# A four-layer stack on one core: biased attention written out over its eight pairs of heads, a state scan with its work moved between engines, and stages whose first loads are put in another order

## The chip, the cores and the metric

The program runs on 1 core of one Trainium2 chip. The metric is the device time of one execution in microseconds (us); lower is better. The engines are TensorE (PE; PEld is its weight load), VectorE (DVE), ScalarE (ACT), GpSimd (POOL) and SyncE (SP, which issues DMAs here, as ACT's queue does too).

## The reference, cut to what matters

Eight sublayers follow each other on 4 x 1024 tokens of width 256, each as x = layernorm(x + f(x)). Four of them touch the change.

```
# L1 attention (stage Catt): 16 heads of width 16, not causal, no mask; bias by distance
P = softmax(q k^T * scale + rel_emb[bucket(mem - ctx)]);  o = P v
# L0 attention (stage Aatt): the same without bias, causal.
# L0 and L3 "ffn" (stages B0*, B1*, H0*, H1*): two layers each of rotary, windowed attention
# (8 heads of width 64, window 128) and a gated MLP.
# L2 attention (stage scan):
phi = k_val[..., None] * theta;  re_k = cos(phi);  im_k = sin(phi)
num_re = cumsum(p_w * re_k);     num_im = cumsum(p_w * im_k)
out_re = sum_m(num_re * qr + num_im * qi) * inv
# L3 attention (stage lru): h_t = lam * h_{t-1} + gamma * B x_t with complex lam, as a scan;
# it needs tables cos(n w), sin(n w) for n < 1024, worked out from a log that is an input.
```

## The kernel before, in words

The program is a chain of 30 stages, one function call each. A stage has its own tiles and semaphores, writes its result to HBM, and ends with a barrier over all engines, so nothing of the next stage runs before the last instruction of this one, and what a stage loads first it loads with every engine idle. Inside a stage each engine has its own program, and waits on semaphores for the others. `pipelined(eng, count, steps, parts)` writes such a program: the parts run in each step with their lags, iteration 0 is written out as instructions with constants, iterations 1 to count-1 are one hardware loop (`Fori`), whose waits take their values from registers, and the lagging parts of the last iteration are written out behind it.

**Thin attention** (`stage_thin_attention`; Aatt without bias, Catt with it). An iteration is a pair of heads, 8 in all, with 64 steps: 4 batches x 2 heads x 8 tiles of 128 query rows. In a step PE makes scores of 128 rows against all keys (L1094), DVE adds the window of biases and takes the negated row maximum (L1155, one per step, into `Catt_nmax`); 24 steps later PE makes the scores again by key with the maximum and the far biases as extra rows of the contraction (L1116), DVE adds the near biases for the blocks beside the diagonal (L1179), ACT takes exp (L1216), and PE sums the values three steps later (L1137). Once in 16 steps the maxima are split in three bf16 parts, turned by PE (L1104), and sent through HBM into rows 96 to 98 of Q. SP loads Q, K, V, and for Catt the extra rows of K (`ext`), `near` and the `win`dows. At the start of the stage POOL fills V and K[96:99] with ones, makes tables and an identity, and raises `set_up`; SP, PE and DVE wait for that, and SP for Catt also for three DMAs (`put`) of the table `of` into Q. One semaphore `head_in` per batch counts all its loads.

**Local attention** (`stage_local_attention`, four stages): the same way, `head_in` counts q, k and V; scores use q and k alone, V comes in five steps later. **Rotary qkv** (`stage_qkv_rotary`, four stages): SP loads the weights w, then the rotary tables and six small rows of scales, all on `w_in`, and then the activations `hT` in the loop; PE and DVE wait for all of `w_in`.

**The state scan** (`stage_state_scan`): 64 steps (4 batches x 2 groups x 8 tiles). In a step DVE makes the phase `ph` (L2353) and its rounded value `nn` (L2357), POOL the fraction f = ph - nn (L2275), ACT |f|, sin and cos (L2323, L2324, L2326), DVE weighs the sines (L2362) and POOL the cosines (L2280), PE runs the two cumulative sums by 16 matmuls of 512 columns (8 where a group starts; L2304, L2306), DVE multiplies both sums by the queries (L2373, twice), POOL adds the products (L2287), DVE reduces (L2378) and scales (L2381). `ph`, `nn`, `f`, `ys` lie in SBUF; only `cum` is in PSUM.

**The recurrence** (`stage_recurrence`, lru): DVE first builds the tables of sines from the logs, a chain of about 130 small instructions ending in L2772, and only then starts on the states (L2783), for which PE has the inputs (L2693).

Of the kernel before, what the change touches and what calls it, by code (L numbers as in the profile page):

```python
# [25 lines left out]
P = 128  # L26
B = 4
# [51 lines left out]
def pipelined(eng, count, steps, parts):  # L79
# [17 lines left out]
    for i in range(steps, steps + max(lag for lag, _ in parts)):  # L97
        run(count - 1, i)

# [187 lines left out]
def stage_enter(nc, x, act0, acts):  # L287

    with ExitStack() as ctx:
        pl = Pool_(nc, ctx, "enter")  # L290
        xin = pl.sb("xin", [P, IN, C])
# [46 lines left out]
        def _(s):  # L338
# [3 lines left out]
            with s.Fori(0, B) as it:  # L342
                for u in range(NT):
# [6 lines left out]
                                xt[:, si, :].rearrange("p (k t) -> p k t", k=KT)).then_inc(cols_out[si], 16)  # L350
            for i in range(IN):
                s.wait_ge(cols_out[i], 16 + 16 * B * NT // IN)

# [267 lines left out]
def stage_local_attention(nc, name, q_s, k_s, v_s, r_s, oT_s, scale):  # L621
# [6 lines left out]
    with ExitStack() as ctx:  # L628
# [14 lines left out]
        head_in = [pl.sem(f"head_in{i}") for i in range(B)]  # L643
# [27 lines left out]
        def _(sp):  # L671
            def load(it, b):
                sp.wait_ge(pv_done, it * ST + (b + 1) * NT)
                apart(sp, pl.sp_unread)
                for i, x in enumerate((q_s, k_s)):
                    sp.dma_start(qk[:, b, i, :], x[bass.ds(it * P, P), b * T:(b + 1) * T]).then_inc(head_in[b], 16)
                sp.dma_start(V[:, b], v_s[b * T:(b + 1) * T, bass.ds(it * P, P)].rearrange("(t p) d -> p t d", p=P)
                             ).then_inc(head_in[b], 16)
# [36 lines left out]
        def _(t):  # L715
# [191 lines left out]
def stage_thin_attention(nc, name, q_s, k_s, v_s, nm_s, r_s, oT_s, scale, bias=None):  # L907
# [6 lines left out]
    causal = bias is None  # L914
    PAIRS, hd, GS, LAG, PRIMED = 8, 16, 16, 24, 16
# [4 lines left out]
    LOADS = 4 if causal else 6  # L920
# [40 lines left out]
    with ExitStack() as ctx:  # L961
# [16 lines left out]
        ident_made, set_up, put = pl.sem("ident_made"), pl.sem("set_up"), pl.sem("put")  # L978
        head_in = [pl.sem(f"head_in{i}") for i in range(B)]
# [19 lines left out]
        def _(sp):  # L999
            sp.wait_ge(set_up, 1)  # L1000
            if not causal:
# [5 lines left out]
                sp.wait_ge(put, 16 * PARTS)  # L1007
# [6 lines left out]
            def load(it, b):  # L1014
                if b == 1 and not causal:
                    window(it, 0)
                sp.wait_ge(pv_done, it * nv + (b + 1) * (nv // B))
                apart(sp, pl.sp_unread)
                for x, x_s in ((Q, q_s), (K, k_s)):
                    sp.dma_start(x[0:K0, b], x_s.rearrange("f t c -> (f t) c")[bass.ds(it * (2 * K0), 2 * K0), b * T:(b + 1) * T]  # L1020
                                 .rearrange("(h p) c -> p h c", h=2)).then_inc(head_in[b], 16)
                for h in range(2):
                    sp.dma_start(V[:, b, :, h, 0:hd], v_s[b * T:(b + 1) * T, bass.ds(it * (2 * hd) + h * hd, hd)]
                                 .rearrange("(t p) d -> p t d", p=P)).then_inc(head_in[b], 16)
                if not causal:
                    sp.dma_start(K[K0 + PARTS:K1, b], ext[bass.ds(it * (2 * PARTS * NT), 2 * PARTS * NT), :]
                                 .rearrange("(h p) c -> p h c", h=2)).then_inc(head_in[b], 16)
                    sp.dma_start(near[:, b], nears[bass.ds(it * (2 * P), 2 * P), :].rearrange("(h p) c -> p h c", h=2)
                                 ).then_inc(head_in[b], 16)
                if b == 1 and not causal:  # L1030
                    window(it, 1)

# [14 lines left out]
        def _(g):  # L1047
            g.memset(V[:], 1.0)
            g.drain()
            g.memset(K[K0:K0 + PARTS], 1.0)  # L1050
            g.drain()
            if causal:
                CausalWindow().make(g, win[:, 0, :])
                g.drain()
# [26 lines left out]
        def _(t):  # L1081
            t.sem_inc(pv_done, nv)
            t.sem_inc(m_turned, 2)
            t.wait_ge(set_up, 1)

            def scores(it, j):
                b, (h, u) = j // GS, row_of(j)
                if j % GS == 0:
                    t.wait_ge(head_in[b], it * (16 * LOADS) + 16 * LOADS)
# [7 lines left out]
            def turn_maxima(it, j):  # L1097
# [3 lines left out]
                n = behind_sums(b)  # L1101
                t.wait_ge(split_done, it * B + (b + 1))
# [4 lines left out]
            def scores_by_key(it, i):  # L1107
                b, h, kb = i // GS, i % 2, i % GS // 2
                if i % GS == 0:
                    t.wait_ge(max_in[b], it * 16 + 16)  # L1110
                if (i + LAG - 3) % GS == GS - 1 and not (isinstance(it, int) and it == PAIRS - 1 and b == B - 1):
# [29 lines left out]
            pipelined(t, PAIRS, ST, ((0, scores), (3, turn_maxima), (LAG, scores_by_key), (LAG + 3, values)))  # L1141

        @block.vector
        def _(v):
            v.sem_inc(masked, ST)
            v.wait_ge(set_up, 1)
# [24 lines left out]
            def add_near(it, i):  # L1171
                b, h, kb = i // GS, i % 2, i % GS // 2
                for c, lo, hi, n, some in units[i]:
# [15 lines left out]
            pipelined(v, PAIRS, ST, ((LAG, add_near), (0, mask), (LAG + 9, invert)))  # L1189
# [1755 lines left out]
```

## Time and profile before

| | |
|---|---|
| time, 3 runs | 8263.17 us median (8258.72 to 8267.3) |
| the profiled execution | 8261.89 us, of it 8260.2 us span |
| busy in the span | PE 82%, DVE 59%, ACT 33%, POOL 19% |
| stage Aatt | 282.3 to 1061.9 us |
| stages B0qkv, B1qkv, H0qkv, H1qkv | from 1173.4, 2011.6, 6559.0 and 7409.6 us, 224 to 226 us each |
| stages B0att, B1att, H0att, H1att | from 1400.6, 2240.2, 6786.7 and 7637.2 us, 243 to 257 us each |
| stage Catt | 3169.7 to 4385.9 us |
| stage scan | 4961.2 to 5588.9 us |
| stage lru | 6337.3 to 6556.5 us |

A share of the span is an average over 30 stages that have different bounds, so the stage must be read, not the total. In the rows below a time is in us from the start of the span; PEclk 1.00 is the clock of 2.4 GHz and 0.50 that of 1.2 GHz. In brackets behind an instruction stands the idle time of its engine before it and what ended it; "issue" is idle time that no other engine or DMA explains.

### The profile page before, as it was taken

The page shows a single profiled execution, that of the slowest core. Times are in us where ns is not written, and L with a number is a line of the kernel's source. Part 1 is how long each engine was busy: PE and PEld are TensorE (multiplying, and loading weights), DVE is VectorE, ACT ScalarE, POOL GpSimd, SP SyncE. Part 2 cuts the span into 40 slices and gives each one's busy share as a digit, 9 for nine tenths or more (in the row PEclk, how much of TensorE's full clock was granted, in tenths as well). Part 3 has the DMA queues.
Part 4 walks back from the last instruction along what each step waited for, and adds up shares of the span by engine and source line. Part 5 has one row for each costly group of instructions (what it writes and reads, how often), then busy time and mean ns, then how long its engine had stood idle before and what let it go on. Part 6 is the DMA issues. An engine that isn't in the chain of part 4 may idle for free. (4 is left out here: it accounts for less than half of the span.)

```text
span 8260.2 us, 122768 instructions
## 1 busy us (share of the span) xinstructions
PE 6734.6 (82%) x30724; PEld 3442.2 (42%) x30724; DVE 4886.6 (59%) x12027; ACT 2733.4 (33%) x6003; POOL 1566.9 (19%) x847
## 2 busy tenths in 40 slices
PE   6799958988898866999994486776886689889989
PEld 3233334554465432222223352334443345544554
DVE  3555557634774535777775749994334676337645
ACT  0255524612471101555551113331110146124621
POOL 1111115100510011000000007880000261006100
PEclk9899979999999987999997698998988899999999
DMA  5322244542454274222223221103001345424541
GB/s 177 95 60 59 52 131 146 172 136 73 149 173 146 81 250 115 72 64 66 64 49 105 82 75 41 30 25 114 23 30 32 101 149 169 139 71 138 172 153 55
DMA packets 921871, 833.01 MB, mean 101 GB/s; under 512 B 239752, under 2 KB 786528, under 8 KB 921248
## 3 DMA queue, kind: packets, MB, share of 16 engines
q1 hardware_dynamic: 491920, 505.95, 21.2%
q10 hardware_dynamic: 429568, 323.08, 12.5%
q14 instruction: 280, 2.29, 0.1%
q8 instruction: 103, 1.69, 0.1%
HBM read 486.33 MB, written 345.74 MB: 101 GB/s over the span
## 5 line engine op out<-in xcount | busy, mean ns | idle before, releaser
L1216 ACT ACTIVATE Catt_E<-Catt_t 128x512 f32<-128x512 f32 x1024 | 576.8, 596 | 501.6 <-DVE Catt_t L1179 319.7
L1155 DVE CUSTOM_DVE_ANT_0 Catt_S<-Catt_s,Catt_win 128x1024 f32<-128x1024 f32 x512 | 621.3, 1215 | 40.9 <-DMA Catt_win<-skewed 38.8
L1155 DVE CUSTOM_DVE_ANT_0 Aatt_S<-Aatt_s,Aatt_win 128x128 f32<-128x128 f32 (+7 forms) x512 | 377.2, 756 | 325.7 <-PE Aatt_s L1094 320.0
L1137 PE MATMUL Catt_o<-Catt_E,Catt_V 128*32 128x256 f32 (+1 forms) x3840 | 548.6, 404 | 0.0
L1216 ACT ACTIVATE Aatt_E<-Aatt_t 128x512 f32<-128x512 f32 (+3 forms) x768 | 355.4, 489 | 325.5 <-PE Aatt_t L1119 257.4
L1179 DVE TENSOR_TENSOR Catt_t<-Catt_t,Catt_near 128x256 f32<-128x256 f32 (+2 forms) x640 | 281.2, 456 | 261.6 <-PE Catt_t L1116 229.9
L1116 PE MATMUL Catt_t<-Catt_Q,Catt_K 123*128 123x512 bf16 x1024 | 327.9, 388 | 91.9 <-ACT Catt_E L1216 71.8
L1094 PE MATMUL Catt_s<-Catt_K,Catt_Q 96*128 96x512 bf16 x1024 | 324.4, 400 | 46.8 <-DMA Catt_near<-near_s 38.1
L2304 PE MATMUL scan_cum<-scan_X,scan_after 128*128 128x512 f32 x448 | 251.3, 644 | 121.8 <-DVE scan_pr L2373 117.5
L1137 PE MATMUL Aatt_o<-Aatt_E,Aatt_V 128*32 128x256 f32 (+2 forms) x2304 | 324.5, 389 | 0.0
L2306 PE MATMUL scan_cum<-scan_X,scan_upto 128*128 128x512 f32 x512 | 279.0, 637 | 39.5 <-POOL scan_X L2280 23.5
L1137 PEld LDWEIGHTS Catt_o<-Catt_E,Catt_V 128*32 128x32 f32 x3840 | 180.3, 110 | 272.0 <-issue 184.3
L1078 POOL TENSOR_TENSOR Catt_O<-Catt_O,Catt_Rb 64x1024 f32<-64x1024 f32 x32 | 75.4, 2357 | 1126.2 <-DMA Catt_Rb<-r_s 1126.2
L1116 PE MATMUL Aatt_t<-Aatt_Q,Aatt_K 99*128 99x512 bf16 (+3 forms) x768 | 241.8, 333 | 48.4 <-ACT Aatt_E L1216 23.6
L1094 PE MATMUL Aatt_s<-Aatt_K,Aatt_Q 96*128 96x512 bf16 (+3 forms) x768 | 219.4, 342 | 42.9 <-DMA Aatt_V<-v_s 26.4
L2275 POOL TENSOR_TENSOR scan_f<-scan_ph,scan_nn 128x1024 f32<-128x1024 f32 x64 | 208.3, 3255 | 46.3 <-DVE scan_nn L2357 46.3
L1116 PEld LDWEIGHTS Catt_t<-Catt_Q,Catt_K 123*128 123x128 bf16 x1024 | 99.4, 98 | 282.3 <-ACT Catt_E L1216 185.4
L1078 POOL TENSOR_TENSOR Aatt_O<-Aatt_O,Aatt_Rb 64x1024 f32<-64x1024 f32 x32 | 75.1, 2347 | 690.5 <-DMA Aatt_Rb<-r_s 690.5
L2323 ACT ACTIVATE scan_ab<-scan_f 128x1024 f32<-128x1024 f32 x64 | 67.7, 1057 | 408.0 <-POOL scan_f L2275 408.0
L2304 PEld LDWEIGHTS scan_cum<-scan_X,scan_after 128*128 128x128 f32 x448 | 86.7, 204 | 256.1 <-issue 232.9
L2580 DVE TENSOR_TENSOR moe_hid<-moe_sg,moe_u 128x512 f32<-128x512 f32 x80 | 54.3, 686 | 223.9 <-ACT moe_sg L2519 223.9
L1094 PEld LDWEIGHTS Catt_s<-Catt_K,Catt_Q 96*128 96x128 bf16 x1024 | 59.3, 98 | 298.3 <-issue 263.2
(724 smaller groups left out, 15070.5 us busy)
## 6 DMA issues: line engine op xcount, KB each, us to landing
bias_rows<-line SPq DMA_DIRECT2D x16, 960.0 KB
skewed<-bias_win ACTq DMA_DIRECT2D x16, 960.0 KB, 5.9
Catt_win<-skewed SPq DMA_DIRECT2D x16, 960.0 KB, 4.7
rec<-state_in_r ACTq DMA_DIRECT2D x32, 416.0 KB, 2.4
scan_r<-rec SPq DMA_DIRECT2D x64, 208.0 KB
Aatt_Q<-q_parts SPq DMA_DIRECT2D x32, 384.0 KB
Aatt_K<-k_parts SPq DMA_DIRECT2D x32, 384.0 KB
Catt_Q<-q_parts SPq DMA_DIRECT2D x32, 384.0 KB
```

The source lines that it names most:

```text
L1078: g.tensor_tensor(o, o, half(Rb, b), ALU.mult).then_inc(o_scaled, 1)
L1094: ins = t.matmul(s_ps[j % 2][:, c:d], Q[0:K0, b, h, u * P:(u + 1) * P], K[0:K0, b, h, c:d], start=True, stop=True)
L1116: ins = t.matmul(t_ps[n % 2][:, 0:hi - lo], K[:, b, h, kb * P:(kb + 1) * P], Q[:, b, h, lo:hi], start=True, stop=not diagonal)
L1137: ins = t.matmul(o_ps[f:f + 2 * hd, x:y], V[:, b, kb, h, :], E[:, kb % NB, h, x:y], start=kb == 0, stop=kb == end and y == hi)
L1155: v.tensor_tensor_reduce(out=S[:, j % 2, 0:w], in0=s_ps[j % 2][:, 0:w], in1=win[:, 0 if causal else h, w0:w0 + w], scale=-1.0, scalar=BIG, ...
L1179: v.tensor_tensor(x, x, near[:, b, h, a - (kb - 1) * P:z - (kb - 1) * P], ALU.add).then_inc(near_done, 1)
L1216: a.activation(E[:, kb % NB, h, lo:hi], t_ps[n % 2][:, 0:hi - lo], ACT.Exp, scale=scale).then_inc(exped, 1)
L2275: g.tensor_tensor(f[:, j % 2, :], ph[:, j % 2, :], nn[:, j % 2, :], ALU.subtract).then_inc(f_done, 1)
L2304: t.matmul(cum[i][:, c:c + 512], after[:], X[:, (j - 1) % 4, i, c:c + 512], start=False, stop=False, skip_group_check=True)
L2306: ins = t.matmul(cum[i][:, c:c + 512], upto[:], X[:, j % 4, i, c:c + 512], start=u == 0, stop=True, skip_group_check=True)
L2323: a.activation(ab[:], f[:, s, :], ACT.Abs)
L2580: ins = v.tensor_tensor(h, sg[:, k % 2, :], u_ps[k % 2][:], ALU.mult)
```

## The change

(1) For Catt, PE, DVE and ACT no longer use `pipelined` but `written_out`: all 512 steps are instructions with constant waits, with no hardware loop. SP and POOL keep their loops, and Aatt keeps `pipelined` on all engines. (2) Thin attention starts differently: K's ones are set by DVE, not POOL; the semaphore `head_in` counts only Q and K, `late_in` the rest; SP no longer waits for `set_up`; for Catt the first window is loaded right behind Q and K of batch 0 and the `put` DMAs are issued behind the second window. (3) Local attention waits for V on its own semaphore. (4) Rotary qkv loads w, then the first two `hT` pieces, then the tables, which have their own semaphore `r_in` that DVE alone waits for. (5) The recurrence's tables are built in the first stage (enter), where DVE had nothing to do, and stay in SBUF; ACT makes the two sines there between batch 0 and batch 1. (6) The scan: `ph` and `ys` go to PSUM; the rounding is an ACT instruction (`whole`, with a bias of 12582912), the fraction a DVE instruction that reads `nn` and the PSUM `ph`; POOL keeps the weighing, one step later and behind DVE's, and the add; the imaginary sum goes first.

```diff
+def written_out(eng, count, steps, parts):
+    for i in range(count * steps + max(lag for lag, _ in parts)):
+        for lag, fn in parts:
+            if 0 <= i - lag < count * steps:
+                fn((i - lag) // steps, (i - lag) % steps)
# stage_enter
+            tables.load(sp, logs)
...
-            with s.Fori(0, B) as it:
+            columns(0)
+            tables.sines(s)
+            with s.Fori(1, B) as it:
+                columns(it)
# stage_local_attention
-                    t.wait_ge(head_in[b], it * 48 + 48)
+                    t.wait_ge(head_in[b], it * 32 + 32)
...
+                if u == 0:
+                    t.wait_ge(V_in[b], it * 16 + 16)
# stage_thin_attention
+    run = pipelined if causal else written_out
...
-            sp.wait_ge(set_up, 1)
-                sp.wait_ge(put, 16 * PARTS)
...
+                if b == 0 and not causal and isinstance(it, int):
+                    window(it, 0)
+                if b == 0 and isinstance(it, int):
+                    sp.wait_ge(V_ones, 1)
...
                 if b == 1 and not causal:
                     window(it, 1)
+                    if isinstance(it, int):
+                        put_of()
...
-            g.memset(K[K0:K0 + PARTS], 1.0)
-            t.wait_ge(set_up, 1)
-                    t.wait_ge(head_in[b], it * (16 * LOADS) + 16 * LOADS)
+                    t.wait_ge(head_in[b], it * 32 + 32)
+                if b == 0 and isinstance(it, int):
+                    t.wait_ge(set_up, 1)                 # before the maxima are turned
+                if i == 0 and isinstance(it, int):
+                    t.wait_ge(K_ones, 1)                 # before the scores by key
+                        t.wait_ge(put, 16 * PARTS)
+                    t.wait_ge(late_in[b], it * (16 * LATE) + 16 * LATE)
-            pipelined(t, PAIRS, ST, ((0, scores), (3, turn_maxima), (LAG, scores_by_key), (LAG + 3, values)))
+            run(t, PAIRS, ST, ((0, scores), (3, turn_maxima), (LAG, scores_by_key), (LAG + 3, values)))
-            v.wait_ge(set_up, 1)
+            v.memset(K[K0:K0 + PARTS], 1.0).then_inc(K_ones, 1)
# stage_qkv_rotary
+            columns(0, 0)
+            sp.dma_start(rt[:], rot.rearrange("(t p) a d -> p t a d", p=P)).then_inc(r_in, 16)
...
+            columns(0, 1)
-            t.wait_ge(w_in, 16 * 8)
+            t.wait_ge(w_in, 16)
-            v.wait_ge(w_in, 16 * 8)
+            v.wait_ge(r_in, 16 * 7)
# stage_state_scan
+        ph = pl.ps("ph", (P, W))
+        ys = [pl.ps(f"ys{i}") for i in range(2)]
-            pipelined(g, B, ST, ((1, weigh), (0, fraction), (2, add)))
+            pipelined(g, B, ST, ((2, weigh), (3, add)))
-                    for i in range(2):
+                    for i in (1, 0):
+            def whole(it, j):
+                a.wait_ge(ph_done, n + 1)
+                a.wait_ge(f_done, n + 1)
+                a.activation(nn[:, j % 2, :], ph[:], ACT.Identity, bias=magic[:]).then_inc(rounded, 1)
-            pipelined(a, B, ST, ((0, trig), (3, store)))
+            pipelined(a, B, ST, ((1, trig), (0, whole), (4, store)))
+            def fraction(it, j):
+                v.wait_ge(rounded, n + 1)
+                v.wait_ge(trig_done, n + 1)
+                v.scalar_tensor_tensor(out=f[:, j % 2, :], in0=nn[:, j % 2, :], scalar=-MAGIC, in1=ph[:],
+                                       op0=ALU.add, op1=ALU.subtract).then_inc(f_done, 1)
             def phase(it, j):
+                v.drain()
...
-                v.drain()
-                v.tensor_scalar(nn[:, j % 2, :], ph[:, j % 2, :], MAGIC, -MAGIC, ALU.add, ALU.add).then_inc(ph_done, 1)
-            pipelined(v, B, ST, ((0, phase), (1, weigh), (2, read), (3, reduce)))
+            pipelined(v, B, ST, ((1, fraction), (0, phase), (2, weigh), (3, read), (4, reduce)))
# stage_recurrence: L2729 to L2773 (exp of the logs, the doubling of the tables) go to
# RecurrenceTables.make(v), which stage_enter's DVE program calls; q.wait_ge(trig_done, 2) goes.
```

## Rows read from the trace of the kernel before

**Rows 1.** Windows: stage Catt and stage scan; busy us (count) of each engine, clock, DMA.

```profile
3169.00:4386.00 1217.00, 1071.33 (x5920) 342.02 (x5920) 886.93 (x1824) 617.39 (x1089) 87.95 (x40) 0.95 0.26 62
4961.00:5589.00 628.00, 464.71 (x960) 191.11 (x960) 598.16 (x449) 203.19 (x193) 503.46 (x197) 0.92 0.11 30
```

**Rows 2.** Timeline: DVE in one step of the scan, and the next step's first.

```profile
5259.61 1.21 DVE L2353 TENSOR_TENSOR scan_ph<-scan_th,scan_r 128x1024 f32<-128x1024 f32 x1
5260.90 2.23 DVE L2357 TENSOR_SCALAR scan_nn<-scan_ph 128x1024 f32<-128x1024 f32 x1
5263.05 1.21 DVE L2362 TENSOR_TENSOR scan_X<-scan_sn,scan_r 128x1024 f32<-128x1024 f32 x1
5264.18 1.21 DVE L2373 TENSOR_TENSOR scan_pr<-scan_cum,scan_r 128x1024 f32<-128x1024 f32 x1
...
5267.80 1.32 DVE L2381 TENSOR_TENSOR scan_y<-scan_ys,scan_r 128x128 f32<-128x128 f32 x1
5269.04 1.21 DVE L2353 TENSOR_TENSOR scan_ph<-scan_th,scan_r 128x1024 f32<-128x1024 f32 x1
```

**Rows 3.** Timeline: POOL in the same step.

```profile
5260.36 2.21 POOL L2280 TENSOR_TENSOR scan_X<-scan_cs,scan_r 128x1024 f32<-128x1024 f32 x1 [0.83 <-ACT scan_cs L2326]
...
5266.60 2.37 POOL L2287 TENSOR_TENSOR scan_pr<-scan_pr,scan_pi 128x1024 f32<-128x1024 f32 x1
```

**Rows 4.** Windows: that step; PE, PEld, DVE, ACT, POOL.

```profile
5259.60:5269.00 9.40, 7.07 (x17) 2.96 (x16) 9.18 (x8) 3.11 (x4) 7.85 (x3) 1.00 0.11 30
```

**Rows 5.** Timeline: the scan's first steps, DVE and ACT.

```profile
4968.73 0.69 DVE L2357 TENSOR_SCALAR scan_nn<-scan_ph 128x1024 f32<-128x1024 f32 x1
...
4973.91 1.28 ACT L2324 ACT_TABLE_LOAD   x1
```

**Rows 6.** Timeline: DVE and PE where pair 1 of Catt jumps back to pair 2.

```profile
3463.25 0.63 DVE L1179 TENSOR_TENSOR Catt_t<-Catt_t,Catt_near 128x128 f32<-128x128 f32 x2 [5.16 <-issue]
...
3464.32 1.09 PE L1116 MATMUL Catt_t<-Catt_Q,Catt_K 123*128 123x512 bf16 x2 [5.41 <-ACT Catt_E L1216]
```

**Rows 7.** Windows of the tile Catt_S alone: DVE busy (count), clock, DMA.

```profile
3287.00:3321.00 34.00, 19.43 (x16) 1.00 0.34 86
3355.20:3389.70 34.50, 19.43 (x16) 1.00 0.26 55
3424.20:3463.70 39.50, 19.42 (x16) 0.97 0.36 98
3321.00:4330.00 1009.00, 544.07 (x448) 0.98 0.26 62
```

**Rows 8.** DMA queues from 3205 to 3321, pair 0 of Catt: transfers, MB, share.

```profile
q8 instruction: 4, 0.07, 0.2%
q14 instruction: 4, 0.03, 0.1%
```

**Rows 9.** Timeline: start of Catt, SP's queue and DVE.

```profile
3198.50 0.38 SPq L1012 DMA_DIRECT2D Catt_win<-skewed  x1
...
3205.48 1.23 DVE L1155 CUSTOM_DVE_ANT_0 Catt_S<-Catt_s,Catt_win 128x1024 f32<-128x1024 f32 x1 [38.75 <-DMA Catt_win<-skewed]
```

**Rows 10.** Timeline: start of Aatt, POOL and DVE.

```profile
284.21 6.92 POOL L1050 MEMSET Aatt_K<- 3x8192 bf16 x1
...
302.86 0.82 DVE L1155 CUSTOM_DVE_ANT_0 Aatt_S<-Aatt_s,Aatt_win 128x640 f32<-128x640 f32 x1 [23.55 <-PE Aatt_s L1094]
```

**Rows 11.** Start of B1qkv: windows, then PE's first in the timeline.

```profile
2012.00:2018.00 6.00, 0.00 (x0) 0.00 (x0) 0.00 (x0) 0.00 (x0) 0.29 (x1) 0.50 0.90 302
...
2026.04 1.19 PE L1536 MATMUL B1qkv_qk<-B1qkv_w,B1qkv_hT 128*128 128x512 f32 x1 [19.44 <-DMA B1qkv_hT<-cols]
```

**Rows 12.** Timeline: PE's first in B0att.

```profile
1411.03 1.23 PE L729 MATMUL B0att_s<-B0att_qk 64*128 64x128 f32 x6 [14.78 <-DMA B0att_V<-v_s]
```

**Rows 13.** Timeline: start of lru, PE's inputs and DVE's first states.

```profile
6344.94 5.37 PE L2693 MATMUL lru_u<-lru_xc,lru_b 128*128 128x512 f32 x7 [12.98 <-DMA lru_xc<-cols]
...
6373.18 1.41 DVE L2783 SCALAR_TENSOR_TENSOR lru_m<-lru_u,lru_ex,lru_rot 128x512 f32<-128x512 f32 x2 [0.17 <-issue]
```

More of the change, by code:

```diff
@@ L977, in stage_thin_attention @@
         o_ps = pl.ps("o", (P, T))
-        ident_made, set_up, put = pl.sem("ident_made"), pl.sem("set_up"), pl.sem("put")
-        head_in = [pl.sem(f"head_in{i}") for i in range(B)]
+        ident_made, V_ones, K_ones, win_made, set_up, put = (pl.sem(n) for n in ("ident_made", "V_ones", "K_ones", "win_made", "set_up", "put"))
+        head_in, late_in = ([pl.sem(f"{n}{i}") for i in range(B)] for n in ("head_in", "late_in"))
         max_in = [pl.sem(f"max_in{i}") for i in range(B)]
@@ L999, in _, with put_of @@
         def _(sp):
-            sp.wait_ge(set_up, 1)
-            if not causal:
+            def put_of():
                 sp.wait_ge(of_made, 1)
@@ L1014, in load @@
             def load(it, b):
-                if b == 1 and not causal:
+                if b == 1 and not causal and not isinstance(it, int):
                     window(it, 0)
@@ L1047, in _ @@
         def _(g):
-            g.memset(V[:], 1.0)
-            g.drain()
-            g.memset(K[K0:K0 + PARTS], 1.0)
+            if causal:
+                CausalWindow().make(g, win[:, 0, :]).then_inc(win_made, 1)
+                g.drain()
+            g.memset(V[:], 1.0).then_inc(V_ones, 1)
             g.drain()
             if causal:
-                CausalWindow().make(g, win[:, 0, :])
-                g.drain()
                 g.memset(near[:], 0.0)
@@ L1172, in add_near @@
                 b, h, kb = i // GS, i % 2, i % GS // 2
+                if i % GS == 0 and not causal:
+                    v.wait_ge(late_in[b], it * (16 * LATE) + 16 * LATE)
                 for c, lo, hi, n, some in units[i]:
@@ L1187, in invert @@
                 v.reciprocal(sums[:, b % 2], sums[:, b % 2]).then_inc(inverted, 1)
-            pipelined(v, PAIRS, ST, ((LAG, add_near), (0, mask), (LAG + 9, invert)))
+            run(v, PAIRS, ST, ((LAG, add_near), (0, mask), (LAG + 9, invert)))
         @block.scalar
@@ L1473, in stage_qkv_rotary @@
         tr_ps = [pl.ps(f"tr{i}") for i in range(2)]
-        made, w_in, tabled = pl.sem("made"), pl.sem("w_in"), pl.sem("tabled")
+        made, w_in, r_in = (pl.sem(n) for n in ("made", "w_in", "r_in"))
         h_in = [pl.sem(f"h_in{i}") for i in range(2)]
@@ L2261, in _ @@
             g.memset(quarter[:], float(np.pi / 2))
+            g.memset(magic[:], MAGIC)
             g.drain()
@@ L2621, in stage_recurrence @@
+def stage_recurrence(nc, act_in, tables, bre, bim, cre, cim, d, out):
     with ExitStack() as ctx:
@@ L2735, in _ @@
-            v.drain()
-            v.tensor_scalar(n3[:, 0:1], n3[:, 0:1], -MAGIC, None, ALU.add)
-            v.drain()
-            rest = ex[:, 1:2]
-            for part in (6.28125, 0.0019350051879882812, float(2 * np.pi - 6.28125 - 0.0019350051879882812)):
-                v.scalar_tensor_tensor(out=wr[:], in0=n3[:, 0:1], scalar=-part, in1=rest, op0=ALU.mult, op1=ALU.add)
-                v.drain()
-                rest = wr[:]
-            v.tensor_scalar(wr[:], wr[:], 3.1415925, -3.1415925, ALU.min, ALU.max)
@@ L2775, in _ @@
-            v.drain().then_inc(trig_done, 1)
             def states(it, c):
@@ L2828, in local_transformer @@
         return y
-    stage_enter(nc, i["L0_attn_x"], a0, acts)
+    kept = ExitStack()
+    tables = RecurrenceTables(nc, kept)
+    stage_enter(nc, i["L0_attn_x"], a0, acts, tables, i["L3_logs"])
     cur = a0
```

190 lines of the change are left out of this document (107 added, 83 removed).

## The prediction, made before the change was run

> **What bounds it now.** I read the timeline for the starts and ends of the stages first, since 30 stages with a barrier between them simply add up, and the change touches twelve of them. The others should keep their times. Next the windows of the two large ones [rows 1]: in Catt PE is busy 1071 of 1217 us and DVE 887; in the scan DVE 598 of 628, PE 465, POOL 503, ACT 203. So Catt belongs to PE and the scan to DVE, and neither share says what the engine does with its time. The timeline of one scan step [rows 2] does: from one `ph` to the next, 9.43 us, with DVE busy 9.18 [rows 4]. Two of its instructions are too long for what they do. `nn` has one operand of 1024 elements and takes 2.23 us, but 0.69 in the first step, when POOL has no work yet [rows 5]; POOL's product `X` runs from 5260.36 to 5262.57, over `nn` [rows 3]. `y`, 128 elements, takes 1.32 while POOL's add runs until 5268.97. So DVE waits inside its instructions for POOL. The products that read `cum` in PSUM take 1.21 beside the same POOL [rows 2]. In Catt I looked at the masks (tile `Catt_S`), 16 to a group [rows 7]: a written-out group takes 34.00 us, a looped one 34.50, and one that holds the jump back 39.50, where DVE and PE both stand for 5 us with nothing that the profile can name [rows 6]. Last, the first work of each stage and what ended the wait ahead of it [rows 9 to 13].
>
> **The scan.** Starts of successive DVE products are 1.13 apart (5263.05 to 5264.18 [rows 2]). From the first `pr` to `y` 3.62 pass; without two reads at 1.13, reduce with its drain has 1.36. A new DVE step is then fraction 1.21, phase 1.13, weigh 1.13, two reads 2.26, reduce 1.36 and `y` 0.25 (128 of 1024 elements of 1.13, and some start, an estimate as its row is a blocked one): 7.34, say 7.4. `nn` leaves DVE, the fraction comes. Does POOL still block it? Fraction, reads and `y` have an operand in PSUM, the kind that row 2 shows unblocked. POOL's product now waits for DVE's weigh, so it lies beside the reads; its add follows the reads and needs 2.4, over reduce, `y` and fraction (2.8). Phase starts just behind it.
> The Trainium skill, SBUF — State Buffer, section "SBUF: two separate sides", says that a DVE instruction in its fast mode or with two SBUF inputs and a GpSimd one exclude each other for a whole instruction. The trace agrees with it for `nn` (2.23 against 0.69); by that rule no pair is left here but phase and weigh, with the sum unchanged.
> The other engines: PE is busy 7.07 in the step [rows 4], now under DVE's 7.4; POOL 2.21 + 2.37 = 4.6 [rows 3]; ACT 3.11 [rows 4] and the new `whole`, some 1.05 (a third of 3.11). The circle fraction, |f| and sines, `whole`, next fraction is 1.21 + 3.11 + 1.05 and some 0.5 of handing over, 5.9. So DVE still sets the step: 64 x (9.43 - 7.4) = 130, less 5 for one more lag to fill: **-125**. Bounds: all six large ones at 1.13 give 7.03, 64 x 2.4 - 5 = -149; -61 is the rival below.
>
> **Catt written out.** Pairs 1 to 7 took 1009.0 for 28 groups [rows 7]. Written-out code shows 34.00; the looped groups next to it 34.50, of which some may be PE's own and stay. I take 34.2: 28 x 34.2 = 958, **-51** (34.0: -57; 34.5: -43). That is 8.5 for each of the six jumps: 5.0 in the group itself (39.50 - 34.50) and the rest behind it, in the looped code's 0.3 a group and in the groups after a jump.
> The Trainium skill, Runtime: NRT & Kernel Launch, section "Instruction fetch mechanics", says that a taken branch out of the held pages must fetch before it goes on, and that straight code is fetched ahead. The rows on the jump agree; by that rule all six go.
>
> **Catt's front.** The first mask waits for `win`, issued at 3198.50 and used at 3205.48 [rows 9], 7 later. The stage starts at 3169.7. SP now waits for nothing, issues Q and K (0.4 each) and the window at some 3171.1, and the first mask is due at 3178 to 3180 against 3205.5: **-26** (20 to 27). What is late next: the `put` DMAs stand in SP's queue behind the second window, so behind the loads of batches 0 and 1, and should land by 3195. PE needs the maxima's parts from step 19 and `put` from step 24; at 34/16 = 2.1 a step that is 3219 and later. DVE's memset of K's ones takes POOL 6.92 [rows 10], at most that on DVE, and lies beside the window's load.
>
> **Aatt's front.** There POOL's two fills stood ahead of SP, and the first mask came 20.6 after the start, at 302.86 [rows 10]. Now Q and K land some 5 after it, and DVE's memset (5 to 6.9) ends at 287.5 to 289.5: mask at some 288.5, **-14.5** (11 to 15).
>
> **Rotary qkv, four times.** The loads run at 302 GB/s with the queues 0.90 busy, mean of the first 6 us, and PE starts at 2026.04, 14.4 after the stage [rows 11]. By their shapes w is 1.57 MB and the first `hT` pieces 0.5: 2.1 MB at 302 is 7 us from 2012, some 2019, PE from 2020.5: -5.5 each. DVE needs the tables for its first product later, and its multiply by the scales then comes about when PE's first results do; if it is late, some is lost: 3.5 to 6.5. **-22** (14 to 26).
>
> **Local attention, four times.** PE's first waited for V [rows 12]. Without V it needs Q and K; at least one issue (0.4), at most 3.5 of V's small rows. I take 2.5: **-10** (1.6 to 14).
>
> **lru.** The states start at 6373.18; the inputs they need are there behind seven or eight matmuls, 6344.94 + 5.37 = 6350 [rows 13]. POOL and ACT had been waiting for the same chain. **-23.5** (20 to 24).
>
> **enter.** ACT paces that stage (63 us) and gets a table load (1.28 [rows 5]) and two short sines, SP one issue of 0.4 ahead: **+2.5** (1 to 4). The doubling of the tables, about 30 us of small DVE instructions, is hidden there, where DVE had nothing; without that cover lru's 23.5 would come back here.
>
> Sum: -125 - 51 - 26 - 14.5 - 22 - 10 - 23.5 + 2.5 = -269.5. The profiled execution took 8261.9, so 7992.4; it lies 1.3 below the median of the runs, so **7994** for those.
>
> **Rivals.** (a) *The scan gets another bound.* ACT gets `whole` behind the sines; a table load is 1.28 [rows 5], and if |f| or `whole` lies in another table, each step has two: the circle is 5.9 + 2.56 = 8.4, over DVE's 7.4. Two DVE instructions blocked for half a us each by POOL would do as much. Gain 64 x (9.43 - 8.4) - 5 = 61 and not 125: 8058. Against: ACT's four instructions per step with |f| among them are busy 3.11 in all [rows 4], so |f| loads nothing. For: phase starts only 0.4 behind the end of POOL's add.
> The Trainium skill, ScalarE: Activation LUTs, section "Table sets: the hidden batching unit", has abs, copy and identity in every set; by that, `whole` loads nothing, and rows 4 agree for |f|.
> (b) *The fronts give nothing*, since the loads are as fast as the queues are (0.90 busy [rows 11]) and the first steps merely wait at another place. Then scan and Catt's jumps alone count, 176: 8087. Against: in Catt, Aatt and lru the wait was for POOL's fills and DVE's chain, not for a transfer's length.
> (c) *Slower: written-out code must be fetched.* Pair 0, which is written out, took 8 instruction fetches [rows 8], so seven more pairs take 56. If each stopped its engine as a jump does, 8.5 with what follows, that were 476: 8263 - 270 + 476 = 8469; it turns the sign from 270/56 = 4.8 each. Against: groups of pair 0 with such fetches took 34.00, the shortest of all [rows 7]. Only if the fetches for PE, DVE and ACT fell behind after pair 0 would this come.
>
> **Numbers.** The main case has 0.64, (a) 0.21, (b) 0.08, (c) 0.03; 0.04 is for more than the bounds allow. The main case's own range is 7952 (all bounds at their best: 149 + 57 + 27 + 15 + 26 + 14 + 24 - 1 = 311) to about 8045 (the scan at 100, the rest at half way to their lower bounds). The range given reaches over (a) to (b): 7950 to 8086. Below 0.2%, 16.5 us, a measurement of this kernel can hardly tell a change from none; only (c) and a stumble inside it come near: faster 0.96, same 0.01, slower 0.03.
>
> **What would show it.** In the scan: `ph` to `ph` 7.4 on DVE, no instruction of it over 1.4, no table load but the first; 8.4 with loads is (a). In Catt: groups of 34.0 to 34.2 throughout, no 5 us of "issue"; groups of 36 and more with fetches inside are (c). First masks 9 after Catt's start and 6 after Aatt's; PE's first 9 after a rotary stage's start and 8 after a local one's; lru's states 13 after its start; enter ending at 66.6. I would be wrong above all if DVE's step were longer for reads of PSUM by two engines at once, or if PE, at half clock after any stall, became the slower one in the scan (7.07 of 7.4 is little room).

## The result and the profile after

The changed kernel takes 7997.63 us, median of 4 runs (7994.45 to 7999.97); before it was 8263.94 in the same series. The ratio is 0.9678, 95% interval 0.9661 to 0.9695. The profiled execution took 7999.97. The forecast was 7994, range 7950 to 8086.

Since the stages only add up, the comparison is made stage by stage. A stage is counted here from its first instruction to the first of the next one, in the timelines of before and after; "forecast" is the term of the prediction.

| stage | before | after | difference | forecast |
|---|---|---|---|---|
| enter | 65.8 | 61.9 | -3.9 | +2.5 |
| Aatt | 782.5 | 773.7 | -8.9 | -14.5 |
| four rotary qkv | 911.1 | 886.4 | -24.7 | -22 |
| B0att | 249.4 | 245.9 | -3.5 | -2.5 |
| B1att | 246.3 | 257.6 | +11.3 | -2.5 |
| H0att, H1att | 521.2 | 513.0 | -8.2 | -5 |
| Catt | 1219.1 | 1139.6 | -79.5 | -77 |
| scan | 630.3 | 510.5 | -119.8 | -125 |
| lru | 221.7 | 202.2 | -19.5 | -23.5 |
| moe (the experts, not edited) | 644.2 | 624.0 | -20.2 | 0 |
| the other 16 stages, not edited | 2767.8 | 2782.7 | +14.9 | 0 |

So the total is right to 4 us, but partly by luck: a stage that nobody edited gave 20, one that should gain lost 11. In these two traces the edited stages give 256.7 together, where 269.5 were forecast, and the unedited ones 5.3. About half of moe's 20 and the whole of B1att's 11 turn out to have one cause, which the prediction did not have (below). Of the 14.9 in the other 16 stages, 9.5 lie in the stage just ahead of the scan; it takes 246.5 to 254.7 in the traces of the kernels below, with the same code, so they may be chance.

First the scan. The timeline of one step after the change, DVE, with ACT's new instruction and POOL's product and add:

```profile
5099.64 1.23 DVE L2407 TENSOR_TENSOR scan_ph<-scan_th,scan_r 128x1024 f32<-128x1024 f32 x1
5100.78 1.22 DVE L2414 TENSOR_TENSOR scan_X<-scan_sn,scan_r 128x1024 f32<-128x1024 f32 x1
5101.92 1.22 DVE L2425 TENSOR_TENSOR scan_pi<-scan_cum,scan_r 128x1024 f32<-128x1024 f32 x1
5102.08 1.90 POOL L2319 TENSOR_TENSOR scan_X<-scan_cs,scan_r 128x1024 f32<-128x1024 f32 x1 [2.79 <-DVE scan_X L2414]
...
5102.94 1.11 ACT L2361 ACTIVATE scan_nn<-scan_ph,scan_magic 128x1024 f32<-128x1024 f32 x1
...
5104.34 2.35 POOL L2326 TENSOR_TENSOR scan_pr<-scan_pr,scan_pi 128x1024 f32<-128x1024 f32 x1 [0.36 <-DVE scan_pr L2425]
5105.47 0.29 DVE L2433 TENSOR_TENSOR scan_y<-scan_ys,scan_r 128x128 f32<-128x128 f32 x1
5105.68 1.21 DVE L2400 SCALAR_TENSOR_TENSOR scan_f<-scan_nn,scan_ph 128x1024 f32<-128x1024 f32 x1
...
5106.98 1.23 DVE L2407 TENSOR_TENSOR scan_ph<-scan_th,scan_r 128x1024 f32<-128x1024 f32 x1
```

From `ph` to `ph` 7.34 us, where it was 9.43 [rows 2]. `y` takes 0.29, not 1.32, though POOL's add runs from 5104.34 to 5106.69 over it, and the fraction takes 1.21 under the same add. Nothing on DVE in this step is longer than 1.23 (in the whole stage two instructions are: one `ph` of 2.31 in the first steps and one `X` of 2.09 near the end), and the stage has one table load. The windows (busy us and count of PE, PEld, DVE, ACT, POOL; clock; DMA), in the order Catt, scan, that step, a longer one, against [rows 1, 4]:

```profile
3160.00:4299.60 1139.60, 1054.05 (x5920) 337.95 (x5920) 890.46 (x1825) 617.12 (x1089) 81.02 (x39) 0.97 0.28 67
4880.00:5391.00 511.00, 437.97 (x960) 182.27 (x960) 465.10 (x449) 274.41 (x257) 273.48 (x134) 0.95 0.13 37
5102.00:5109.50 7.50, 7.15 (x18) 3.00 (x17) 7.33 (x8) 4.42 (x5) 4.33 (x3) 1.00 0.14 38
5159.20:5168.30 9.10, 8.23 (x20) 3.53 (x19) 8.69 (x10) 4.39 (x5) 5.55 (x3) 1.00 0.15 36
```

PE is busy 7.15 of 7.5, so it has become a near second bound, and in seven of the 63 steps it is the first: they take 8.8 to 9.4. PE's timeline at one of them (a start of a group of tiles), and the windows that say what clock it was granted:

```profile
5148.03 2.08 PE L2343 MATMUL scan_cum<-scan_X,scan_after 128*128 128x512 f32 x2 [3.75 <-DVE scan_pi L2425]
5149.90 1.75 PE L2345 MATMUL scan_cum<-scan_X,scan_upto 128*128 128x512 f32 x2
5151.48 1.02 PE L2343 MATMUL scan_cum<-scan_X,scan_after 128*128 128x512 f32 x2
```

```profile
5143.00:5148.00 5.00, 1.28 (x3) 0.21 (x2) 4.91 (x6) 3.37 (x4) 2.13 (x2) 0.99 0.20 56
5148.00:5151.50 3.50, 3.47 (x5) 1.52 (x6) 3.43 (x4) 0.90 (x1) 3.21 (x2) 0.52 0.00 0
5152.00:5158.00 6.00, 6.00 (x16) 2.65 (x15) 4.49 (x5) 4.04 (x4) 1.90 (x1) 1.00 0.10 35
5088.40:5091.90 3.50, 3.42 (x8) 1.63 (x9) 3.43 (x4) 0.85 (x1) 3.14 (x2) 1.00 0.00 0
```

Where a group of tiles starts PE has 8 matmuls and not 16. It stands 3.75 us, and behind that the granted clock is 0.52 (1.2 GHz) for 3.5 us, two matmuls take 2.08 and not 1.02, and in the step after, DVE's `pr` waits 1.51 for the sums. PE stands 3.7 to 3.8 us at seven group starts of the stage. Behind six of them the granted clock is 0.53 to 0.67 for the next 3.5 us, and the step takes 9.1 to 9.4; behind the seventh, at 5088.48 (last row), the clock stays at 1.00 and the step takes 7.45. So, as far as these seven show, what costs is the clock behind the stand and not the stand itself; why it stayed up once is open. (The seventh long step, 8.8, is at the very start of the stage.)

Catt: two groups of masks (the windows of tile `Catt_S`), the last of pair 0 and the one that held the first jump before, against [rows 7]:

```profile
3255.40:3289.30 33.90, 19.37 (x16) 1.00 0.35 87
3391.20:3425.30 34.10, 19.43 (x17) 1.00 0.34 86
```

All groups of pairs 1 to 7 take 33.8 to 34.6. The fronts, in DVE's timeline of Catt and then of Aatt, against [rows 9, 10]:

```profile
3161.88 6.88 DVE L1178 MEMSET Catt_K<- 3x8192 bf16 x1 [4.85 <-issue]
3168.88 1.23 DVE L1189 CUSTOM_DVE_ANT_0 Catt_S<-Catt_s,Catt_win 128x1024 f32<-128x1024 f32 x1
...
3183.60 1.22 DVE L1189 CUSTOM_DVE_ANT_0 Catt_S<-Catt_s,Catt_win 128x1024 f32<-128x1024 f32 x1 [4.79 <-DMA Catt_win<-skewed]
```

```profile
283.28 6.88 DVE L1178 MEMSET Aatt_K<- 3x8192 bf16 x1 [4.93 <-issue]
290.20 0.82 DVE L1189 CUSTOM_DVE_ANT_0 Aatt_S<-Aatt_s,Aatt_win 128x640 f32<-128x640 f32 x1
```

In both stages the fill of K's ones, 6.88 us on DVE as it was 6.92 on POOL, ends just ahead of the first mask: what the prediction hid behind the loads is now the last thing that the mask waits for. In Catt the ninth mask also waits 4.79 for the second window.

The surprise is in B1att, in DVE's timeline before and after at the same point of the program, the jump back from one pair to the next. Before, the work goes on:

```profile
2357.70 0.69 DVE L668 COPY B1att_PT<-B1att_pt 128x512 f32<-128x512 f32 x1 [0.31 <-PE B1att_pt L741]
2358.38 0.29 DVE L782 CUSTOM_DVE_ANT_0 B1att_S<-B1att_s,B1att_win 128x128 f32<-128x128 f32 x1
```

After the change it doesn't:

```profile
2333.18 0.69 DVE L687 COPY B1att_PT<-B1att_pt 128x512 f32<-128x512 f32 x1 [0.31 <-PE B1att_pt L760]
2339.47 0.29 DVE L803 CUSTOM_DVE_ANT_0 B1att_S<-B1att_s,B1att_win 128x128 f32<-128x128 f32 x1 [5.59 <-issue]
```

This loop was not edited; its body is 350 DVE instructions in both. What changed is how much DVE code lies ahead of it: enter now holds the tables' chain. What DVE waits for is code. The queue listing of the second round, from one jump to the next, shows no transfer of instructions before:

```profile
q1 hardware_dynamic: 6859, 11.26, 63.9%
```

and after the change, for the same round:

```profile
q1 hardware_dynamic: 6791, 11.01, 57.4%
q14 instruction: 5, 0.04, 0.2%
```

One of those five starts inside the first jump, at 2337.22, and one more, at 2399.35, inside the second. So before, the loop ran its round without fetching anything, and after the change every round fetches, with DVE standing at the jump.

### The profile page after: what moved, and what is told of

Read it like the earlier page. It is cut to its first block and busy times, and to the rows that moved or that the text cites. A ratio compares the mean times of both kernels' runs of the same rounds, so it can differ in the third digit from the quotient of the medians.

```text
span 7998.3 us, 119081 instructions
## 1 busy us (share of the span) xinstructions
PE 6696.7 (84%) x30724; PEld 3430.9 (43%) x30724; DVE 4761.2 (60%) x12029; ACT 2802.8 (35%) x6066; POOL 1323.1 (17%) x782
## 5 line engine op out<-in xcount | busy, mean ns | idle before, releaser
L1148 PE MATMUL Catt_t<-Catt_Q,Catt_K 123*128 123x512 bf16 x1024 | 321.6, 382 | 51.8 <-ACT Catt_E L1252 33.8
L2528 PE MATMUL moe_g<-moe_xc,moe_wg 128*128 128x512 f32 x320 | 166.6, 645 | 0.0
L2345 PEld LDWEIGHTS scan_cum<-scan_X,scan_upto 128*128 128x128 f32 x512 | 99.3, 195 | 154.7 <-issue 151.8
L2326 POOL TENSOR_TENSOR scan_pr<-scan_pr,scan_pi 128x1024 f32<-128x1024 f32 x64 | 150.8, 2356 | 40.0 <-DVE scan_pr L2425 40.0
```

Of the source, the lines that this page charges most:

```text
L1148: ins = t.matmul(t_ps[n % 2][:, 0:hi - lo], K[:, b, h, kb * P:(kb + 1) * P], Q[:, b, h, lo:hi], start=True, stop=not diagonal)
L2326: g.tensor_tensor(pr[:, m % 2, :], pr[:, m % 2, :], pi[:, m % 2, :], ALU.add).then_inc(sum_done, 1)
L2345: ins = t.matmul(cum[i][:, c:c + 512], upto[:], X[:, j % 4, i, c:c + 512], start=u == 0, stop=True, skip_group_check=True)
L2528: ins = t.matmul(ps[k % 2][:], w[:, kt, j * P:(j + 1) * P], xc[:, c, kt, :], start=kt == 0, stop=kt == KT - 1)
```

## The experiments

Times are medians. The kernel before took 8253 to 8264 in the different series, so differences under 10 us between kernels of different series are judged by the stage in the trace; the ratios to before stand where the total matters. There is one trace of each kernel. A stage with the same code differs by some us from trace to trace: Aatt takes 772.2 to 776.6 in those that leave it as the change has it, the scan 509.2 to 513.4, Catt 1138.7 to 1141.3.

**Which engine's jump?** In Catt PE, DVE and ACT are put back on `pipelined` together, DVE alone, or PE and ACT without DVE.

```diff
-            run(v, PAIRS, ST, ((LAG, add_near), (0, mask), (LAG + 9, invert)))
+            pipelined(v, PAIRS, ST, ((LAG, add_near), (0, mask), (LAG + 9, invert)))
```

All three looped: 

> The changed kernel with one part undone: in stage Catt PE, DVE and ACT loop over the pairs again; scan and fronts stay new. In the changed kernel's trace the 28 groups of pairs 1 to 7 take 950 us in place of 1009, so the theory that the jumps and the looped code were worth this everywhere expects 7998 + 59 = 8057 (8050 to 8062), with six groups of 39.5 again. The rival, that part of the gain came from the new front (other places of the loads against the groups), expects clearly less, 8030 or below.

DVE alone: 

> The changed kernel with DVE alone looping over the pairs in Catt; PE and ACT stay written out. In the trace before, DVE shows 5.1 us from the branch to its next instruction, ACT 2.7, PE 0.2, and PE's wait was ended by ACT, which waited for DVE. Theory: DVE's jump alone is what the stage pays; then this costs nearly all of it, 8050 to 8057, groups with the jump at 39.5. Rival: every engine's jump adds its part; then it lies at half or less, 8020 to 8035. What the other groups take (34.5 or 34.0) tells whose looped waits the 0.5 was.

PE and ACT: 

> The counterpart: PE and ACT loop over the pairs in Catt, DVE alone is written out. Theory (DVE's jump is the one that counts): 7998 to 8010, no group over 36, since ACT's 2.7 and PE's 0.2 fit into what the buffers between the engines hold. Rival (every jump adds): ACT's 2.7 with the half clock behind it six times and the looped groups' 0.5 give 8020 to 8035.

Measured 8061.15, 8056.85 and 8002.67 (one of the last kernel's four executions took 8103). Catt itself took 1193.2, 1187.5 and 1148.5 against 1139.6: +53.6, +47.8 and +8.8. DVE's timeline where it jumps in the second kernel, with PE and ACT written out:

```profile
3419.75 0.63 DVE L1215 TENSOR_TENSOR Catt_t<-Catt_t,Catt_near 128x128 f32<-128x128 f32 x2 [5.09 <-issue]
```

and the windows of the masks for a group with the jump in that kernel and, with DVE written out, in the third:

```profile
3381.00:3420.30 39.30, 19.46 (x17) 0.98 0.36 98
```

```profile
3386.70:3420.90 34.20, 19.42 (x16) 1.00 0.34 86
```

So the jump of DVE alone was what the 5.4 us of PE [rows 6] waited for. ACT's own jump is 2.4 to 2.8 long, from its branch to its next instruction, and the group that holds it takes no longer than the others; the group behind it takes up to 0.6 more. With its waits looped on PE and ACT the third kernel takes some 0.3 more a group (34.1 to 34.9). The rest of the total in the first two kernels is for the most part moe: 634.4 and 635.8 and not 624.0, and DVE's jump there is 2.8 us in both and 0.3 in the third, where DVE's code ahead of it is as long as in the changed kernel. In the two main traces it is the same: 2.8 before, 0.3 after. The queues agree: a round of moe has five transfers of instructions in the trace of before and in loop_all's, and none after the change.

**Is it where the loop lies?** The first DVE instruction of the loop is placed at the start of a block of 256, in the four local stages and in the looped Catt (and, since the code is shared, in Aatt). PE and ACT are looped in Catt as in the first kernel above. The edit in short form:

```diff
-    with eng.Fori(1, count) as it:
+    with eng.bass.Fori(1, count, engines=bass.OrderedEngineSet([eng.engine]), head_slot={eng.engine: 0}) as it:
```

> Catt looped on all three engines as in loop_all, but the first instruction of DVE's loop is put at the start of a block of 256 instructions, in Catt and in the four local stages. Observed so far: DVE's jump costs 0.3 us or 5 to 6 with the same body (350 instructions: 0.3 in B1att before, 6.1 after the change, whose code lies 229 instructions further). Theory: a body that lies in two blocks is not fetched again; then Catt's body of 465 and the local ones of 350 jump in 0.3: against loop_all's 8061 Catt gives back 6 x 8 = 48, the three slow local stages 3 x 11 = 33, less up to 2.7 for entering each of five loops: 7980 to 7995. Rival: bodies over 256 instructions are always fetched again and B0att's 0.3 has another cause; then 8055 to 8065. Second rival: entering costs what the jumps give.

8044.16, between the two (one of its four executions took 13378 us, which nothing here explains). For the bodies of 350 the theory holds: every jump back in the four local stages takes 0.3, and H0att 244.3, where the first kernel above had 260.1. B1att's round from jump to jump has no transfer of instructions again:

```profile
q1 hardware_dynamic: 6667, 10.57, 61.3%
```

But coming into the loop costs 6.7 once in B1att and H1att (the second rival in part: 252.1 and 251.4). For Catt's body of 465 it fails: its jump still takes 5.1, a round still has instruction transfers, and entering costs 5.5 more (stage 1206.6). So it is not enough that a body fits in two blocks; what decides between 350 and 465 stays open.
The Trainium skill, Runtime: NRT & Kernel Launch, section "Instruction fetch mechanics", says that most engines hold 512 instructions in two blocks of 256, and that a taken branch whose target is outside the two blocks held must fetch it first. The local stages agree (0.3 or 5.9 for one body, by its place). If the two blocks held are simply the last two used, Catt's body of 465 at the start of a block should jump freely; it took 5.1, and there the measurement decides.

**Is it a fetch that could begin earlier?** The same DVE loops with a hint as first instruction of each round, which names the branch at its end; nothing is placed. The edit in short form:

```diff
-    with eng.Fori(1, count) as it:
+    with eng.bass.Fori(1, count, engines=bass.OrderedEngineSet([eng.engine]), hint_back_edge=True) as it:
```

7980.53, ratio 0.9671 (0.9656 to 0.9685): a Catt that is looped on all three engines, and yet a kernel as fast as the changed one. DVE's timeline at the jump in Catt:

```profile
3404.11 0.17 DVE L1204 TENSOR_TENSOR Catt_parts<-Catt_rest,Catt_parts 128x16 bf16<-128x16 f32 x1
3404.71 0.63 DVE L1216 TENSOR_TENSOR Catt_t<-Catt_t,Catt_near 128x128 f32<-128x128 f32 x2 [0.42 <-issue]
```

0.42 in place of 5.16 [rows 6]. The fetch has not gone, it has moved: the queues show instruction transfers at 3461.3 and 3461.5 in the trace of before, inside the jump that begins at 3458.0, and at 3401.1 and 3403.1 here, ahead of the jump at 3404.2. The four local stages take 245.6, 244.5, 245.9 and 244.3, all alike now. Catt takes 1153.7: of the 53.6 that writing out is worth, the hint gets 39.6 without it.

**What frees DVE in the scan: the engine or the memory?** Two kernels each move one buffer of the changed scan back to SBUF.

```diff
-        ph = pl.ps("ph", (P, W))
+        ph = pl.sb("ph", [P, W])
```

> The changed kernel with ph of the scan in SBUF in place of PSUM, nothing else. In the changed kernel's trace the fraction starts at 5105.68 and POOL's add runs to 5106.69. Theory: with both operands in SBUF the fraction is held until the add ends, 1.0 us, the step goes from 7.40 to 8.4, 64 x 1.0: 8060 (8045 to 8070). Rival: the gain came from moving work between the engines, the place of ph doesn't matter: 7995 to 8003.

```diff
-        ys = [pl.ps(f"ys{i}") for i in range(2)]
+        ys = [pl.sb(f"ys{i}", [P, P]) for i in range(2)]
```

> The changed kernel with ys of the scan in SBUF, nothing else. y starts at 5105.47 with 0.29 us of work, POOL's add runs to 5106.69. Theory: y is held for 1.2 us as it was before the change (1.32 there), the step goes to 8.6: 7998 + 77 = 8075 (8060 to 8085). Rival: an operand of 128 elements is not held, or its wait is taken back by a later slack: 7995 to 8010.

8046.98 and 8049.92. The fraction in the first and `y` in the second, each beside POOL's add in that kernel's timeline:

```profile
5104.72 2.35 POOL L2326 TENSOR_TENSOR scan_pr<-scan_pr,scan_pi 128x1024 f32<-128x1024 f32 x1 [0.36 <-DVE scan_pr L2425]
5105.92 0.29 DVE L2433 TENSOR_TENSOR scan_y<-scan_ys,scan_r 128x128 f32<-128x128 f32 x1
5106.12 2.02 DVE L2400 SCALAR_TENSOR_TENSOR scan_f<-scan_nn,scan_ph 128x1024 f32<-128x1024 f32 x1
```

```profile
5105.10 2.35 POOL L2326 TENSOR_TENSOR scan_pr<-scan_pr,scan_pi 128x1024 f32<-128x1024 f32 x1 [0.36 <-DVE scan_pr L2425]
5106.22 1.37 DVE L2433 TENSOR_TENSOR scan_y<-scan_ys,scan_r 128x128 f32<-128x128 f32 x1
```

The fraction becomes 2.02 and not 1.21, `y` 1.37 and not 0.29; the steps are 8.23 and 8.42 and not 7.40. That is 0.83 and 1.02 a step, where 1.0 and 1.2 were expected. The stage took 559.6 and 565.6, +49 and +55, and not 64 times those (53 and 65). The first four steps of the stage, which POOL's add does not reach, stay as they were, so only 59 steps grow: 59 times 0.83 is the 49. With `ys` in SBUF the 59 steps would give 60; all but the first of the group starts then lose less to PE than before (9.0 to 9.4 in a step of 8.42), which takes 5 back. So of the 120 us, 49 hang on `ph` lying in PSUM and 55 on `ys`; both at once were not tried, and no run takes the other 16 apart.
The rule of the Trainium skill, SBUF — State Buffer, section "SBUF: two separate sides", that two SBUF inputs against a GpSimd instruction exclude each other for its whole length, is borne out: the add ends at 5107.07 and 5107.45, and the held instructions end at 5108.14 and 5107.59, their own 1.21 and 0.29 behind it, less 0.15.

**The clock at the group starts.** PE makes the first tile's matmuls twice.

```diff
+                            else:
+                                t.matmul(cum[i][:, c:c + 512], upto[:], X[:, j % 4, i, c:c + 512], start=True, stop=True,
+                                         skip_group_check=True)
```

> The changed kernel; where a group of eight tiles starts, PE makes each of its 4 matmuls of 512 columns twice (the first is overwritten), so that it has as many as in every other step. Observed: in those eight steps PE stands 3.75 us and the matmuls behind take 0.78 each in place of 0.51; DVE's step there is 9.1 in place of 7.4. Theory: the stand is what lowers the granted clock and the late sums cost the 1.7; without it the eight steps take 7.4: -12 (7984 to 7989). Rival: the long step has another cause (the first products of a group), 7996 to 8000; or the extra matmuls are late themselves, above 8000.

7989.65; the scan took 502.9, that is -7.6 (the total's ratio, 0.9681, can't show so little). PE no longer stands where groups start, and those steps now take 7.3 to 7.7, so the stand with the low clock behind it was their cause. The forecast of 12 was too much, since the first steps of the stage became longer (one of 9.2 and one of 8.4 where there had been 5.8 and 8.8).

**The fronts.** K's ones on POOL behind its tables, and the second window behind the first.

```diff
-            v.memset(K[K0:K0 + PARTS], 1.0).then_inc(K_ones, 1)
+            g.memset(K[K0:K0 + PARTS], 1.0).then_inc(K_ones, 1)      # POOL, behind set_up
...
                     window(it, 0)
+                    window(it, 1)
```

> The changed kernel; in both thin attention stages POOL sets K's ones behind its tables in place of DVE ahead of its first mask, and Catt's second window is issued right behind the first. Observed: DVE's fill takes 6.88 and the first mask follows it at once (3168.88; in Aatt at 290.20, while PE's scores are there from 287); the ninth mask of Catt waits 4.8 for the second window. Theory: Aatt 3 shorter, Catt 5 shorter (its first mask then waits for the first window or scores at about 3168.2): 7990 (7987 to 7993). Rival: the first mask waits for the transfers just as long, or the V, ext and near loads come late at step 24 in place of them: 7996 to 8000.

7988.81. Aatt 770.8 (-2.9) and Catt 1136.6 (-3.1), each just below what the same code took in any other trace; in the two kernels below, which have this edit too, Aatt takes 768.6 and 768.5 and Catt 1134.8 and 1136.9. In Catt the first mask now waits for the window itself:

```profile
3160.59 1.23 DVE L1192 CUSTOM_DVE_ANT_0 Catt_S<-Catt_s,Catt_win 128x1024 f32<-128x1024 f32 x1 [11.69 <-DMA Catt_win<-skewed]
```

and the first group of masks takes 21.0 in place of 25.7.

**The stages add up.** The changed kernel with the old scan (its function as before). 

> The changed kernel with the scan of before; all else stays new. The stage took 630.3 from its start to the next stage's before and 510.5 after, so 7998 + 120 = 8118 (8112 to 8124) if the stages simply add up, which is the theory. Rival: the stages behind it (a barrier, but the clock may carry over) give some of it back or take some, more than 6 either way.

8116.58; the scan took 629.9, the stages behind it 1 to 3 more or less. They add up, within what a stage differs from trace to trace.

**Together.** front_ones, scan_busy and, in the local stages, first the placing and then the hint. 

> The changed kernel with three additions: front_ones, scan_busy (-8) and DVE's loop at the start of a block in the four local stages (against the changed kernel B0att -1.6, B1att -5.5, H0att -11.6, H1att -5.7 in loop_slots' trace, -24). If they add up: 7998 - 8 - 8 - 24 = 7958 (7952 to 7966). Rival: shifted code behind the local stages puts another loop across blocks (the experts' stage, 2.8 for each jump, 10 to 20 in all): 7968 to 7978.

> best_slot with the hint of loop_hint in place of the block placing in the four local stages (Catt stays written out). In loop_hint's trace those stages took 245.6, 244.5, 245.9 and 244.3 against 245.9, 257.6, 255.9 and 257.1 in the changed kernel, -36; with front_ones -9 and scan_busy -8: 7945 (7938 to 7953), 13 under best_slot, whose loops in B0att, B1att and H1att each pay 5.5 for entering. Rival: the placing and the hint are worth the same in the end: 7955 to 7962.

7958.52 and 7940.08 (ratio to before 0.9622, interval 0.9605 to 0.9640). The local stages are 244.0, 244.7, 246.2 and 244.4. The last kernel's interval lies under the changed one's, by 0.56% in the ratio, 46 us (58 in the two medians). That it beats the one with the placing is not shown: the intervals of the two ratios overlap (0.9625 to 0.9651 there); only the local stages' 979.3 against 999.1 in the traces speaks for it.

## Why the prediction was right, and where it was not

**The scan, right in mechanism and nearly in size.** DVE's step was to be 7.4 and alternates between 7.34 and 7.45. That operands in PSUM keep a DVE instruction free of POOL is shown, by scan_ph and scan_ys. The place where it gave less, 120 for 125, is the one that the text named last: PE at half clock after a stand, in six of the seven long steps.

**Catt written out, right in size (-57 of pairs 1 to 7 for -51), incomplete in cause.** DVE's six jumps and what follows them are 47.8 of it, the looped code of PE and ACT 8.8. But the prediction spoke of "the jump" as if DVE and PE both paid; it is DVE's alone. The value taken for a group, 34.2, was 0.2 too high. Rival (c) did not come: the queues show 82 instruction fetches between 3225 and 4274, and the groups are the shortest of all.

```profile
q8 instruction: 45, 0.74, 0.3%
q14 instruction: 37, 0.30, 0.1%
```

**Catt's and Aatt's fronts, one step failed.** (No run puts a front back; what follows is read from the timelines, and so are the paragraphs on rotary qkv, lru and enter.) "DVE's memset ... lies beside the window's load" was so in Catt only because the load was as long; the first mask came 8.9 after the stage's start, as forecast (9), but behind the fill. What was missed is the second window, 4.8 late: -26.9 at the first mask, 5 given back within the group. For Aatt the estimate of 5 to 6.9 for the fill hid its start: it began 1.9 after the stage's start, so it ended at 8.7 and not at 6. The first mask gained 11.8 and the stage 8.9.

**Rotary qkv**, right: PE's first 8.3 after B1qkv's start, forecast 9, and DVE's multiply at 2009.10 was hidden by PE's 5.51 of first products.

**Local attention, wrong sign in B1att.** The first products came 1.6 to 3.7 earlier in the stages, as forecast (2.5), but the stage lost 11.3 by its two jumps of 5.9 and 6.1 where they had been 0.3. The step that failed is none of the terms: the prediction took every loop that it didn't edit to jump back as before ("the others should keep their times", it says of the unedited stages). Code that is added on an engine moves the loops behind it.

**moe, -20.2, not forecast**: DVE's jumps in it went from 2.8 to 0.3 without an edit. In the kernels where they are back (loop_all, loop_dve, loop_slots, loop_hint) the stage takes 634 to 636. The other 8 to 10 of before's 644 go with a lower granted clock in its loop (0.91 before, 0.93 in loop_all, 0.94 after); why it was lower is open.

**lru, 4 less than forecast.** The states started 13.4 after the stage's start, as forecast, 22.5 earlier than before; the end of the stage kept 3 of it. The same code takes 200.9 to 205.3 in the other traces, always more than the 198.2 that the forecast comes to; what holds the end up is open.

**enter, wrong sign.** The two sines were to add a table load. Before, ACT loaded its table in each of four rounds; now it has two loads in all, as the groups of ACT's lines in enter show, before and then after:

```profile
L347 ACT ACT_TABLE_LOAD x4 | 5.1, 1283 | 26.2 <-PE enter_tp L334 25.1 <-issue 1.1
```

```profile
L357 ACT ACT_TABLE_LOAD x1 | 1.3, 1283 | 1.2 <-ACTq L351 1.2
...
L2687 ACT ACT_TABLE_LOAD x1 | 1.3, 1283 | 0.4 <-ACT enter_xt L357 0.4
```

Two loads less are 2.6 us, which would be most of the 3.9, if ACT paces the stage as the prediction took it; no run shows it apart. The row was there to be read and wasn't.

## What to carry to other kernels

Read the end of each loop's round on each engine: idle time "by issue" of 2.5 to 3 or 5 to 7 us at a jump was a fetch of code here, and the queues show it as instruction transfers inside the round; it depends on how long the body is and where it lies, and any edit ahead of it can bring it or take it away; try the hint at the loop's head before writing the loop out. When DVE and GpSimd share a stage, look for DVE instructions that are longer than their kind, and ask which operand could lie in PSUM. Compare every stage, also those that the change leaves alone.

## What the runs showed of the hardware that was not expected

- One and the same DVE loop of 350 instructions jumps back in 0.3 us or in 5.3 to 6.8, by its place in the program; one of 465 took 4.8 to 5.3 at each of the three places tried; moe's of 308 took 0.3 or 2.7 to 3.0. Where the jump took 0.3 without a hint, the round had no instruction transfer (B1att before, 2357.8 to 2413.7; moe after, 5948.3 to 6098.4). PE's jumps were 0.1 to 0.3, ACT's in Catt and Aatt 2.4 to 2.8.
- With the hint at the loop's head the jumps of both bodies took 0.3.
- A stand of PE of 3.75 us was followed by 3.5 us at a granted clock of 0.52; one of 3.79 by 3.5 us at 1.00.
- An operand in PSUM in place of SBUF took the fraction beside POOL's add from 2.02 to 1.21 us, and the 128-element product from 1.37 to 0.29.
- DVE fills three rows of 8192 bf16 in 6.88 us, GpSimd in 6.92: as a fill alone it is the same length on either.
